# A windowed-attention and mixture-of-experts layer on one core: TensorE's order in an attention step, and the place where the next stage's weights are loaded

## The reference

```python
x = x + attn(_layernorm(x), Wq, bq, Wk, bk, Wv, bv, Wo, bo)       # 16 heads of 16
x = x + ffn(_layernorm(x), gate_w, Wg, Wu, Wd, Sg, Su, Sd)        # 16 experts, I = 1024
...
scores = einsum('bhqd,bhkd->bhqk', Q, K) * scale + longformer_mask(S)   # |i-j| <= 64, token 0 global
out = einsum('bhqk,bhkd->bhqd', softmax(scores), V)
...
topk_weight, topk_idx = top_k(softmax(x @ gate_w.T).T, C)          # C = 512 tokens for each expert
eo = (gelu(xg @ Wg.T) * (xg @ Wu.T)) @ Wd.T * topk_weight           # added back to its tokens
shared = (gelu(x @ Sg.T) * (x @ Su.T)) @ Sd.T
```

## Time and profile before

| what | us |
|---|---|
| median of 3 runs (lowest, highest) | 1303.22 (1300.46, 1308.63) |
| the profiled execution's own time | 1303.8 |
| its span, first to last instruction | 1302.1 |
| attention's steps, first exponents to the last copy of `ps_o` (140.5 to 443.5) | 303 |
| from there to the shared expert's first product (443.5 to 486.9) | 43.4 |
| the rest of `front` and all experts (486.9 to the end) | 815 |
| mean granted TensorE clock | 0.952 |

### The profile page before, as it was taken

How to read it: one execution, slowest core, us unless ns; L and a number is a source line. 1 busy time by engine, 2 the same in 40 slices (tenths; PEclk the granted TensorE clock), 3 DMA queues, 4 the chain that set the end, 5 groups by cost and what they waited for, 6 DMA issues and landing times. The chain is left out here.

```text
span 1302.1 us, 23565 instructions
## 1 busy us (share of the span) xinstructions
PE 1170.8 (90%) x8906; PEld 971.9 (75%) x8906; DVE 859.4 (66%) x2182; ACT 597.7 (46%) x959; POOL 642.7 (49%) x794
## 2 busy tenths in 40 slices
PE   0997799999999448999986899999999999999997
PEld 0885566666666337988875688888888888888886
DVE  7895577777777056647886866666767666666641
ACT  1340466666656424443221545444555554554442
POOL 8000355555555445522000476677666666676754
PEclk9997799999999867899998899999999999999999
DMA  2589476786764366310031444344444444344311
GB/s 91 199 285 146 122 118 110 112 128 115 119 112 86 106 206 178 98 53 20 30 130 41 158 126 129 94 118 127 124 130 123 117 109 123 105 129 118 96 30 17
DMA packets 62349, 149.08 MB, mean 114 GB/s; under 512 B 14992, under 2 KB 31776, under 8 KB 52896
## 3 DMA queue, kind: packets, MB, share of 16 engines
q1 hardware_dynamic: 49584, 128.72, 38.3%
q0 software_dynamic: 12656, 18.90, 8.1%
HBM read 104.73 MB, written 42.34 MB: 113 GB/s over the span
## 5 line engine op out<-in xcount | busy, mean ns | idle before, releaser
L572 DVE CUSTOM_DVE_ANT_0 junk_s<-ps_s,mask 128x258 bf16<-128x258 f32 (+2 forms) x512 | 213.9, 470 | 86.5 <-PE ps_s L649 83.2
L1806 POOL TENSOR_TENSOR h_lo<-h,h_hi 128x512 fp32r<-128x512 f32 x128 | 179.0, 1410 | 117.8 <-ACT h_hi L1842 117.5
L626 ACT ACTIVATE pt<-ps_p 128x516 f32<-128x516 f32 (+2 forms) x256 | 167.3, 680 | 112.9 <-PE ps_p L673 62.1
L1916 PE MATMUL ps_gu<-xt_hi,w_hi 128*128 128x512 f32 x512 | 202.9, 396 | 2.1 <-DVE xt_lo L1865 2.1
L479 POOL TENSOR_SCALAR_AFFINE_SELECT pt<-pt 128x256 f32<-128x256 f32 x352 | 133.8, 416 | 140.3 <-ACT pt L626 140.2
L1916 PE MATMUL ps_gu<-xt_lo,w_hi 128*128 128x512 f32 x512 | 200.1, 391 | 0.0
L1916 PE MATMUL ps_gu<-xt_hi,w_lo 128*128 128x512 f32 x512 | 199.9, 390 | 0.0
L1881 DVE TENSOR_TENSOR h<-ge,ps_gu 128x512 f32<-128x512 f32 x128 | 87.8, 686 | 168.5 <-ACT ge L1836 152.1
L1743 DVE TENSOR_TENSOR w_lo<-w,w_hi 128x768 fp32r<-128x768 f32 x128 | 174.0, 1364 | 31.3 <-ACT w_hi L1738 27.8
L1815 POOL DMA_INDIRECT out<-ys,idx x64 | 139.7, 2182 | 71.7 <-ACT ys L1852 57.7
L649 PE MATMUL ps_s<-ks,qs 96*128 96x258 f32 (+2 forms) x512 | 148.7, 348 | 12.0 <-PEq L191 9.0
(11 more groups left out here) (221 smaller groups left out, 2429.7 us busy)
## 6 DMA issues: line engine op xcount, KB each, us to landing
w<-in_We SPq DMA_DIRECT2D x48, 1024.0 KB, 4.9
qk_parts<-qk SPq DMA_DIRECT2D x8, 2064.0 KB, 7.8
qs<-qk_parts SPq DMA_DIRECT2D x96, 129.0 KB, 3.8
ks<-qk_parts SPq DMA_DIRECT2D x96, 129.0 KB, 5.6
x<-in_x SPq DMA_DIRECT2D x16, 512.0 KB, 8.1
attn_t<-on SPq DMA_DIRECT2D x32, 256.0 KB, 5.7
ot<-attn_t SPq DMA_DIRECT2D x16, 256.0 KB, 5.0
rd<-rden SPq DMA_DIRECT2D x16, 256.0 KB, 4.1
```

What stands on the lines that cost most here:

```text
L572: dve.tensor_tensor_reduce(junk[:, (u * SG + g) % RING, 0:n], ps_s[:, (u * SG + g) % RING, 0:n], m, 1.0, -3e38, ALU.add, ALU.max, mx[:, u ...
L626: act.activation(dst, src, ACT.Exp, scale=SCALE).then_inc(exp_s, 1)
L1806: pool.tensor_tensor(h_lo[:, m], h32[:, (e * KI + m) % HB], h_hi[:, m].bitcast(F32), ALU.subtract).then_inc(hlo_s, 1)
L1916: last = pe.matmul(ps_gu[:, m % 2, n], l, r, start=c == 0, stop=c == 3 * KD - 1)
```

## The change

There are two changes. In attention, TensorE's step is written out in single scores, and each of the four value products has a place of its own:

```diff
+                def ahead(u, g):
+                    if u + 2 < NU:
+                        score(u + 2, g)
+                def behind(u, i):
+                    if u >= 1:
+                        times_v(u - 1, i)
+                def step(u):
+                    ahead(u, 0)
+                    exponents(u, 0)
+                    ahead(u, 1)
+                    ahead(u, 2)
+                    exponents(u, 1)
+                    ahead(u, 3)
+                    ahead(u, 4)
+                    exponents(u, 2)
+                    behind(u, 0)
+                    ahead(u, 5)
+                    ahead(u, 6)
+                    ahead(u, 7)
+                    exponents(u, 3)
+                    exponents(u, 4)
+                    behind(u, 1)
+                    ahead(u, 8)
+                    ahead(u, 9)
+                    ahead(u, 10)
+                    exponents(u, 5)
+                    behind(u, 2)
+                    ahead(u, 11)
+                    ahead(u, 12)
+                    exponents(u, 6)
+                    ahead(u, 13)
+                    behind(u, 3)
+                    exponents(u, 7)
+                    ahead(u, 14)
+                    ahead(u, 15)
...
                 for u in range(NU):
-                    for n in range(SJ):
-                        if n not in (1, 5):
-                            scores(u + 2, n)
-                        exponents(u, n)
-                        if n in (0, 4):
-                            scores(u + 2, n + 1)
-                            if u >= 1:
-                                times_v(u - 1, n // 2)
-                                times_v(u - 1, n // 2 + 1)
+                    step(u)
```

```diff
+        PIECES = [(OW_AT, OW_AT + OWC, OWC)] + [(PIECE * c, SWC + PIECE * c, PIECE) for c in range(4)]
+        PIECE_AT = {6 + 3 * c: c for c in range(len(PIECES))}
...
                     near_only(u, 3)
+                    if u - 1 in PIECE_AT:
+                        c = PIECE_AT[u - 1]
+                        hi, lo, n = PIECES[c]
+                        pool.wait_ge(piece_hi, c + 1)
+                        pool.tensor_tensor(held[:, lo:lo + n], staged(c), held[:, hi:hi + n].bitcast(F32),
+                                           ALU.subtract).then_inc(piece_lo, 1)
...
+                def load_piece(c):
+                    if c == 0:
+                        for h in range(2):
+                            sp.wait_ge(qk_out[h], 16 * (B // 2))
+                        sp.dma_start(staged(0)[:, 0:KD * D].rearrange("p (k n) -> p k n", k=KD), d["Wo"]).then_inc(piece_in, 16)
+                        sp.dma_start(staged(0)[:, KD * D:OWC].rearrange("p (k n) -> p k n", k=KD), d["gate"]).then_inc(piece_in, 16)
+                        sp.dma_start(stage[:, 0:D], d["bo"]).then_inc(bo_in, 16)
+                    else:
+                        sp.wait_ge(piece_lo, c)
+                        sp.dma_start(staged(c), d["Sw"][:, PIECE * (c - 1):PIECE * c]).then_inc(piece_in, 16)
...
                         store(u - 2)
+                    if u in PIECE_AT:
+                        load_piece(PIECE_AT[u])
...
+                        if n == 3 and u - 1 in PIECE_AT:
+                            c = PIECE_AT[u - 1]
+                            act.wait_ge(piece_in, LANDED[c])
+                            act.activation(held[:, PIECES[c][0]:PIECES[c][0] + PIECES[c][2]], staged(c), ACT.Copy).then_inc(piece_hi, 1)
```

In `front` the loads, splits and waits of these weights are gone, and the low parts of the first two sequences' outputs are made by DVE instead of POOL:

```diff
@@ front, POOL
-                for dst, src in ((wo32, "Wo"), (ga32, "gate"), (bo[:], "bo")):
-                    pool.dma_start(dst, d[src]).then_inc(w_in, 16)
-                for dst, src in ((sw32, "Sw"), (blk[:], "blk"), (before[:], "before")):
-                    pool.dma_start(dst, d[src]).then_inc(sw_in, 16)
-                pool.wait_ge(w_in, 48)
-                parts(0)
                 biased(0)
-                parts(1)
                 biased(1)
-                pool.wait_ge(swhi, 1)
-                pool.tensor_tensor(sw_lo[:], sw32, sw_hi[:].bitcast(F32), ALU.subtract).then_inc(swlo, 1)
+                for dst, src in ((blk[:], "blk"), (before[:], "before")):
+                    pool.dma_start(dst, d[src]).then_inc(sums_in, 16)
@@ front, ACT
-                act.wait_ge(w_in, 48)
-                act.activation(wo_hi[:], wo32, ACT.Copy).then_inc(whi, 1)
-                act.activation(ga_hi[:], ga32, ACT.Copy).then_inc(whi, 1)
                 ot_part(0)
                 ot_part(1)
-                act.wait_ge(sw_in, 48)
-                act.activation(sw_hi[:], sw32, ACT.Copy).then_inc(swhi, 1)
@@ front, DVE
                 divide(0)
-                dve.wait_ge(whi, 2)
-                dve.tensor_tensor(wo_lo[:], wo32, wo_hi[:].bitcast(F32), ALU.subtract).then_inc(wlo, 1)
-                dve.tensor_tensor(ga_lo[:], ga32, ga_hi[:].bitcast(F32), ALU.subtract).then_inc(wlo, 1)
+                ot_low(0)
                 divide(1)
+                ot_low(1)
@@ front, PE
-                pe.wait_ge(wlo, 2)
                 wo(0)
                 wo(1)
                 transposes(0)
-                pe.wait_ge(swlo, 1)
```

## The result

The changed kernel takes 1285.87 us (median of 4 runs, 1281.97 to 1287.65) beside 1302.83 us before (median of 4, 1300.46 to 1308.63): a ratio of 0.986, with a 95% interval of 0.982 to 0.990. It is faster by 1.4%. The forecast was 1275, with a range of 1257 to 1291. The profiled execution took 1285.9 us, with a span of 1283.9.

What follows compares the result with a forecast made beforehand. No engine is full; each waits for another in every attention step, TensorE least. From 1303.8 us: minus 20.5 (attention), plus 3.6 (late rows), minus 11.2 (`front`) gives 1275.7, stated as 1275; range 1257 to 1291.

Steps and rivals of the forecast that it cites:

- dear turns: Rival, attention: at 0.60 us a visit to value products the step stays 9.47, only `front` gains; 1292.6 us; chance 0.13.
- What goes and what comes in a step: Attention step: 1.20 us of waits go, two more visits at 0.28 add 0.56; 9.47 becomes 8.83, 20.5 us gained.
- What becomes late: Attention: `far_rows` and its exponential come about 0.6 us late in six steps behind stores of reciprocals; 3.6 us lost.
- the rival of the slow loop: Attention: row DMAs land 5.6 us after issue, making `exponents(u + 1, 0)` late in every step; 1322.6 us; chance 0.05.
- The pieces at nothing: Attention: five pieces of moved weights (ACT copies, POOL subtractions, SP issues) fit in idle time and cost nothing.
- The rival that saw 11.9 us in attention: Weights only moved: their copies and subtractions show in attention at their full 11.9 us; 1287.6 us; chance 0.12.
- The beginning of `front`: `rd` lands sooner (5.3 us), low part on DVE gains nothing, first Wo product to shared expert 5.9; together 11.2 us.
- The gain passes through to the end: Behind the beginning of `front` the order is the same, so its gain reaches the end; change there 0.
- What I had said would show it: Signs: step 8.8 us, weight loads' wait for DVE under 8 us, `hn` 1.4, shared expert's first product 32 us after last `ps_o` copy.
- cheap ones: Rival, attention: a visit costs 0.10 us, the step 8.47, gaining 32 us instead of 20.5; 1265.6 us; chance 0.20.

Runs made afterwards that it cites:

- e6_split_visits: `e1_no_block` with each value product's halves parted by a score, so eight turns to 32-column products a step instead of four; 1302.44 us, ratio 1.001.
- e1_no_block: Changed kernel, but SP waits for the store of reciprocals only ahead of the next load of denominators, not right behind the store; 1269.24 us, ratio 0.976.
- e3_weights_alone: Changed kernel with the old order of TensorE in attention, so only the weights are moved; 1294.84 us, ratio 0.994.
- e5_loads_first: `e1_no_block`, but in a sequence's second step SP issues the six qs and ks loads ahead of the four row DMAs; 1300.45 us, ratio 0.996.
- e2_order_alone: Kernel before with TensorE's new order alone, weights still loaded at the beginning of `front`; 1293.81 us, ratio 0.989.

## Why the prediction was right, and where it was not

The side was right, and the median lies inside the range, but 11 us above the forecast. That it is still inside is in part luck: the upper end of the range stood for dear turns, and the time was lost elsewhere. By its own steps:

- **What goes and what comes in a step: right.** The forecast step was 9.47 - 1.20 + 0.56 = 8.83; it is 8.73. A visit costs 0.30 (`e6_split_visits`), not 0.28, so the waits that went are 9.47 - 8.73 + 0.60 = 1.34 us, not 1.20. That the waits depend on the places of the value products is shown by the three orders with fewer places. With SP out of the way attention takes 281.0 us instead of 303.0, a gain of 22.0 where 20.5 stood in the sum.
- **What becomes late: the step that failed.** The text has "There are six such steps: 3.6 us lost, between 0 and 9 (1.5 each)" and "In the other steps the row DMAs start right after the turn, some 2.3 us earlier, and fit". The loss is 295.1 - 281.0 = 14.1 us, beyond the upper bound: some 5.6 (6.9 - 1.3) in the six steps themselves, where 3.6 stood, 6.3 in the steps behind them and 2.4 in step 14, where nothing stood. The first part (rows late behind the store) was named; missing was that SP's wait also delays the six loads, so that the rows, and one piece of weights, of the step behind it stand in the queue behind them. I had counted what SP issues, as late as it was, but not what its lateness pushes in front of the next issue. The mechanism was even there, as the rival of the slow loop (a landing of 5.6 us), but with the condition that it would come in every step; it came in the steps behind a store.
- **The clock: not in the sum.** In steps 13 and 14 of after TensorE is busy 2 x (11.13 - 8.73) = 4.8 us longer for the same work, at granted clocks of 0.80 and 0.76. I had priced every stop at its own length.
- **The pieces at nothing: right where SP is not late**, by `e1_no_block` (with the pieces, 8.73 to 8.78 us a step). Where one stands behind late loads, it stops TensorE: 1.31 us in step 13 of after, and 3.6 us with the clock in `e3_weights_alone`. "I cost them all at nothing" left that out. The rival that saw 11.9 us in attention is out.
- **The beginning of `front`: right**, 11.5 for 11.2. `rd` and `divide(0)` gave 4.4 of 5.3, the low part on DVE cost 0.1 (0 forecast), and from the first Wo product to the shared expert it was 7.2 instead of 5.9. `ot_low(0)` took 2.66 us, from 448.00 until 1.1 us after `biased(0)` on POOL had ended at 449.57; the second one took 1.22. The prediction had read the 7.76 us of `hn` as its example, but `hn` has one tensor as input (x, beside two values for each partition), and `ot_low(0)` has two. That is the rule of SBUF — State Buffer, section Who interferes with whom, in the Trainium skill, that the prediction cited: the rows agree. Alone it would have let the first Wo product start some 1.4 us sooner.
- **The gain passes through to the end: right, as far as the runs tell.** The 4.8 us that the rest of `front` took longer are in the main TensorE's: its same 1266 products keep it busy for 207.7 us there instead of 204.2. In five of the seven other runs with the new beginning this stretch takes 219.6 to 223.9 us, at a granted clock of 0.93 to 0.95; in two it takes 227.3 and 227.4, at 0.92 like after. In the two others with the old beginning it takes 222.8 and 222.9. So the loss does not come with the new beginning each time; whether it comes more often is open.
- **What I had said would show it.** The weight loads' wait for DVE is 16.2 us, not under 8, and 17.2 in `e1_no_block`, though the step is 8.73 us there. Part of these waits are put down to DVE and are not DVE's: in `e1_no_block` the load for the first score behind value products begins with that score, at 275.18, when the value products ahead of it end (0.67 us, as in `e6_split_visits`), and DVE had ended at 275.0. The distances between TensorE's rows tell what a step loses; I should have named these, and neither the loads' waits nor the busy share.

The rival of dear turns is out (0.30 a visit, not 0.60), and so is that of cheap ones.

## What to carry to other kernels

When a loop gets shorter, follow each in-order queue once round the loop and into the next turn: a wait that the old step covered delays not only what stands behind it, but puts that in front of the next urgent transfer. A wait for a store to land belongs where its buffer is used again, not behind its issue. And price a stop of TensorE with the stretch behind it, since the clock may fall there.

## What the runs showed that I had not expected

- **The clock falls after short stops inside a full loop.** The five stops of 2.6 to 3.7 us in `e5_loads_first` and four stops of 1.3 to 1.9 us (steps 12 and 13 of after, 12 of `e2_order_alone`, 13 of `e3_weights_alone`) were followed by steps with a granted clock of 0.55 to 0.85, which cost 1.4 to 5.5 us each. It was not so after every stop: `e2_order_alone` stopped for 2.0 us in step 17 and after for 1.26 in step 16, and the clock of the next step stayed at 1.00. In `e1_no_block`, without stops, no step fell.
- **The experts became 3 to 4 us faster.** In all eight profiled runs with the moved weights they take 588.9 to 589.7 us, in the three without 592.6 or 592.7. An expert takes 35.4 us instead of 35.6, and the rows show the down product: 280 ns instead of 283.

```profile
L1933 PE MATMUL ps_y<-w_lo,h_hi x512: 281/283/283, 749.4 to 1293.4; 128*128 128x256 f32 x171
```
```profile
L1979 PE MATMUL ps_y<-w_lo,held x512: 277/280/283, 734.5 to 1275.3; 128*128 128x256 f32 x171
```

The first row is of before, the second of after (shortest, median and longest in ns). The stage's code differs only in where `h_hi`, `h_lo` and one `ys` lie in memory. But `held` and `stage` are allocated ahead of its other tensors, so these may lie elsewhere too. Which of these moves it is was not tried, and the cause is open.
